# Fourth stage of a transformer kernel: products in three rounded parts instead of float32

## The reference

```python
topk_w, topk_idx = jax.lax.top_k(probs, TOP_K)
topk_w = topk_w / jnp.sum(topk_w, axis=-1, keepdims=True)
def expert_step(acc, ws):
    gw, uw, dw, ce = ws
    out = jax.nn.silu(x @ gw) * (x @ uw) @ dw
    return (acc + ce[:, None].astype(out.dtype) * out, None)
...
shared = jax.nn.silu(x @ s_gate_w + s_gate_b) * (x @ s_up_w + s_up_b) @ s_down_w + s_down_b
```

## Time and profile before

| | |
|---|---|
| median of three runs | 1208.76 us |
| profiled execution | 1218.6 us, span 1216.7 us |
| TensorE busy | 1056.7 us (87% of the span) |
| VectorE busy | 479.6 us (39%) |
| ScalarE busy | 341.5 us (28%) |
| GpSimd busy | 386.3 us (32%) |
| gate and up of the fourth stage, line 561 | 624 records, 193.2 us |
| down of the fourth stage, line 577 | 234 records, 107.1 us |

### The profile page before, as it was taken

The page is one execution under the profiler, slowest core; times in us unless marked ns, Lnnn a source line. Parts: engine busy times, 40 slices in busy tenths (PEclk is TensorE's granted clock), DMA queues, the critical chain, the costliest instruction groups (busy, mean ns, idle before and its releaser), DMA issues.

```text
span 1216.7 us, 13055 instructions
## 1 busy us (share of the span) xinstructions
PE 1056.7 (87%) x4351; PEld 705.6 (58%) x4351; DVE 479.6 (39%) x1148; ACT 341.5 (28%) x537; POOL 386.3 (32%) x340
## 2 busy tenths in 40 slices
PE   5886698979979989995599899999089999999996
PEld 4333243469869778884385657675055655565553
DVE  5678757333424544332854644515011111111110
ACT  3464141023323433332243332311012222221221
POOL 0004767525435445453002020202013332333232
PEclk9788699989989999997699999999589999999999
DMA  9111011179989998965406120209913323332330
GB/s 330 70 52 43 11 62 36 51 275 277 260 274 263 263 242 234 246 159 84 159 18 57 47 44 9 52 18 307 320 48 64 62 54 62 68 63 54 64 70 8
DMA packets 52800, 148.52 MB, mean 122 GB/s; under 512 B 12243, under 2 KB 12627, under 8 KB 47296
## 3 DMA queue, kind: packets, MB, share of 16 engines
q1 hardware_dynamic: 24752, 81.09, 21.0%
q0 software_dynamic: 24160, 44.03, 18.8%
q10 hardware_dynamic: 3824, 22.57, 5.8%
HBM read 109.76 MB, written 41.08 MB: 124 GB/s over the span
## 4 chain that ended last, share of the span: by engine, by line
PE 63%; DMA 16%; DVE 10%; issue 4%; ACT 3%; POOL 3%; ACTq 0%; SPq 0%; POOLq 0%; DVEq 0%
PE pb L561 15%; PE pb L577 8%; DMA acc_rows<-big 7%; PE pb L449 7%; PE pb L534 5%; DMA big<-hn_rows,big 5%; PE pb L308 4%; PE pb L310 4%; PE pb L309 4%; DVE big L874 4%; PE pb L315 3%; PE pb L403 3%; PE pb L371 3%; POOL acc_rows L1284 2%; DMA list_rows<-big 2%
## 5 line engine op out<-in xcount | busy, mean ns | idle before, releaser
L561 PE MATMUL pb<-big 128*128 x624 | 193.2, 463 | 4.1 <-issue 4.1
L449 PE MATMUL pb<-big 128*128 128x192 f32 x1024 | 174.1, 329 | 2.1 <-ACT bigr L721 1.3
L449 PEld LDWEIGHTS pb<-big 128*128 128x128 f32 x1024 | 169.8, 192 | 6.4 <-issue 3.4
L561 PEld LDWEIGHTS pb<-big 128*128 128x128 f32 x624 | 116.6, 192 | 63.4 <-issue 6.2
L1253 POOL DMA_INDIRECT list_rows<-big x96 | 95.8, 998 | 137.2 <-DVE big L886 108.5
L1284 POOL DMA_INDIRECT acc_rows<-big x64 | 95.4, 1491 | 138.2 <-DMA acc_rows<-big 53.5
L308 PE MATMUL pb<-bigr 128*128 128x512 f32 (+2 forms) x320 | 132.9, 415 | 7.0 <-DVE big L882 4.6
L1311 POOL DMA_INDIRECT out<-big x39 | 61.8, 1584 | 207.4 <-ACT big L854 207.4
L310 PE MATMUL pb<-bigr 128*128 128x512 f32 (+2 forms) x320 | 127.6, 399 | 0.0
L309 PE MATMUL pb<-bigr 128*128 128x512 f32 (+2 forms) x320 | 127.1, 397 | 0.0
L874 DVE TENSOR_TENSOR big<-big,pb 128x352 f32<-128x352 f32 (+4 forms) x87 | 33.4, 383 | 206.5 <-ACT big L848 192.4
(11 more groups left out here) (119 smaller groups left out, 1167.8 us busy)
## 6 DMA issues: line engine op xcount, KB each, us to landing
big<-in_we SPq DMA_DIRECT2D x32, 1024.0 KB, 8.0
rawr<-in_we SPq DMA_DIRECT2D x32, 512.0 KB, 4.4
big<-in_we ACTq DMA_DIRECT2D x1, 8704.0 KB, 41.5
hn_rows<-big SPq DMA_DIRECT2D x32, 256.0 KB, 2.0
big<-in_we ACTq DMA_DIRECT2D x1, 6528.0 KB, 54.4
big<-in_x SPq DMA_DIRECT2D x4, 1024.0 KB, 15.3
acc_rows<-big SPq DMA_DIRECT2D x16, 256.0 KB, 4.2
big<-acc_rows SPq DMA_DIRECT2D x16, 256.0 KB, 4.8
```

What stands on the lines that cost most here:

```text
L449: r = e.matmul(ps[:, m * CAP:(m + 1) * CAP], WR[b % 4][:, at_:at_ + 128], XT[b % 2][:, k, :], start=(k == 0), stop=(k == 3))
L561: r = e.matmul(ps[:, 0:I1], XT1[b % 2][:, k, :], W1[:, bass.ds(r0 + (q * 4 + k) * I1, I1)], start=(k == 0), stop=(k == 3))
```

## The change

Only the fourth stage is edited. ScalarE rounds each tile's operands and VectorE takes the remainders: the transposed tokens (`XH1`, `XL1`), the gate, up and down weights of the tile's expert (`wgh` and `wgl`, `wuh` and `wul`, `wdh` and `wdl`) and the transposed inner product (`NTH`, `NTL1`). There is one buffer for each of the weights' parts. The register is now loaded by ScalarE and by VectorE instead of TensorE. `upt` is cut in `gatet` and `upt`, and gate, up and down go through `three`. The gathers get a third buffer and semaphores of their own, and are issued three tiles ahead; many small tiles move to other places in SBUF. `IN1` is widened to 384 columns and its end zeroed (`zero4`), so that all three blocks have 128 rows.

```diff
-POOL_3 = "scatter1.0 scatter1.1 scatter1.2 scatter1.3 lists1 fetcht.0 fetcht.1"
+POOL_3 = "scatter1.0 scatter1.1 scatter1.2 scatter1.3 lists1 fetcht.0 fetcht.1 fetcht.2"
...
+        WGH, WGL = SLOT(RING + 9216, 4 * I1), SLOT(RING + 9216 + 4 * I1, 4 * I1)
+        WUH, WUL = SLOT(RING + 2048, 4 * I1), SLOT(RING + 2048 + 4 * I1, 4 * I1)
+        WDH1, WDL1 = SLOT(RING + 5120, 3 * D), SLOT(RING + 5120 + 3 * D, 3 * D)
...
-        pe4 = "turnt.0 " + words(lambda n: f"upt.{n} " + (f"turnt.{n + 1} " if n + 1 < NT else "") + (f"downt.{n - 1} " if n else "") + f"flipt.{n}", NT) + f" downt.{NT - 1}"
-        act4 = "turnt.0 " + words(lambda n: f"silut.{n} " + (f"turnt.{n + 1} " if n + 1 < NT else "") + (f"yt.{n - 1}" if n else ""), NT) + f" yt.{NT - 1}"
-        dve4 = words(lambda n: f"mult.{n} flipt.{n}", NT)
-        pool4 = words(lambda n: (f"fetcht.{n + 2} " if n + 2 < NT else "") + (f"addt.{n - 1}" if n else ""), NT) + f" addt.{NT - 1}"
+        pe4 = "turnt.0 " + words(lambda n: f"gatet.{n} upt.{n} " + (f"turnt.{n + 1} " if n + 1 < NT else "") + (f"downt.{n - 1} " if n else "") + f"flipt.{n}", NT) + f" downt.{NT - 1}"
+        act4 = "turnt.0 wgh.0 wuh.0 " + words(lambda n: f"silut.{n} " + (f"wgh.{n + 1} turnt.{n + 1} wuh.{n + 1} " if n + 1 < NT else "")
+                                              + (f"yt.{n - 1} " if n else "") + f"wdh.{n} flipt.{n}", NT) + f" yt.{NT - 1}"
+        dve4 = "zero4 turnt.0 wgl.0 wul.0 " + words(lambda n: f"mult.{n} " + (f"wgl.{n + 1} turnt.{n + 1} wul.{n + 1} " if n + 1 < NT else "")
+                                                    + f"wdl.{n} flipt.{n}", NT)
+        pool4 = words(lambda n: (f"fetcht.{n + 3} " if n + 3 < NT else "") + (f"addt.{n - 1}" if n else ""), NT) + f" addt.{NT - 1}"
...
-                    r0 = regs[b] = e.value_load(ETK[0:1, b:b + 1], min_val=0, max_val=7 * WE1)
-                    for q, ps in ((0, pg), (1, pu)):
-                        for k in range(4):
-                            r = e.matmul(ps[:, 0:I1], XT1[b % 2][:, k, :], W1[:, bass.ds(r0 + (q * 4 + k) * I1, I1)], start=(k == 0), stop=(k == 3))
-                    r.then_inc(s_pe, c.up())
+                elif kind in ("gatet", "upt"):
+                    q = 0 if kind == "gatet" else 1
+                    wh, wl = ((WGH, WGL), (WUH, WUL))[q]
+                    e.wait_ge(s_dve, dv("turnt", b))
+                    e.wait_ge(s_dve, dv("wgl" if q == 0 else "wul", b))
+                    if b >= 2:
+                        e.wait_ge(s_dve, dv("mult", b - 2))
+                    three(e, PB[2 + 2 * (b % 2) + q][:, 0:I1], [(XH1[b % 2][:, k, :], XL1[b % 2][:, k, :], wh[:, k * I1:(k + 1) * I1], wl[:, k * I1:(k + 1) * I1])
+                                                               for k in range(4)]).then_inc(s_pe, c.up())
...
+                elif kind in ("wgh", "wuh", "wdh"):
+                    at_, n, dst, user = dict(wgh=(0, 4 * I1, WGH, "gatet"), wuh=(4 * I1, 4 * I1, WUH, "upt"), wdh=(8 * I1, 3 * D, WDH1, "downt"))[kind]
+                    if b == 0:
+                        e.wait_ge(l_w1, 64)
...
+                    else:
+                        e.wait_ge(s_pe, pe(user, b - 1))
+                    if kind == "wgh":
+                        regs[b] = e.value_load(ETK[0:1, b:b + 1], min_val=0, max_val=7 * WE1)
+                    prev()
+                    e.activation(dst, w1[:, bass.ds(regs[b] + at_, n)], ACT.Copy).then_inc(s_act, c.up())
...
+                elif kind == "turnt":
+                    e.wait_ge(s_act, av("turnt", b))
+                    if b >= 2:
+                        e.wait_ge(s_pe, pe("upt", b - 2))
+                    tensor(XL1[b % 2].rearrange("p a b -> p (a b)"), PB[0][:, :], XH1[b % 2].rearrange("p a b -> p (a b)").bitcast(F32), ALU.subtract)
+                elif kind in ("wgl", "wul", "wdl"):
+                    at_, n, hi, lo, user = dict(wgl=(0, 4 * I1, WGH, WGL, "gatet"), wul=(4 * I1, 4 * I1, WUH, WUL, "upt"), wdl=(8 * I1, 3 * D, WDH1, WDL1, "downt"))[kind]
+                    e.wait_ge(s_act, av(kind[0:2] + "h", b))
+                    if b:
+                        e.wait_ge(s_pe, pe(user, b - 1))
+                    if kind == "wgl":
+                        regs[b] = e.value_load(ETK[0:1, b:b + 1], min_val=0, max_val=7 * WE1)
+                    tensor(lo, w1[:, bass.ds(regs[b] + at_, n)], hi.bitcast(F32), ALU.subtract)
...
-                    copy(NT1[b % 2][:, 0:2, :].rearrange("p a b -> p (a b)"), PB[1][:, 0:256])
-                    copy(NT1[b % 2][0:96, 2, :], PB[1][0:96, 256:384])
+                    e.wait_ge(s_act, av("flipt", b))
+                    tensor(NTL1[b % 2], PB[1][:, 0:384], NTH[b % 2].bitcast(F32), ALU.subtract)
```

More of the change, by code:

```diff
@@ L118, in program @@
         rawr = second_name("rawr", 17152, 34816, F32)
+        later = second_name("later", 38144, 53120, F32R)
+        slots = second_name("slots", 40192, 50176, F32R)
+        with nc.sbuf_tensor("w1", [128, 34816], F32) as w1:
+            pass
         big = ctx.enter_context(nc.sbuf_tensor("big", [128, 53120], F32))
@@ L133, in R, with LR, SLOT @@
             return S(off - 13056, *shape, mem=bigr)
+        def LR(off, *shape):
+            return S(off - 38144, *shape, mem=later)
+        def SLOT(off, *shape):
+            return S(off - 40192, *shape, mem=slots)
         def RAW(off, *shape):
@@ L227, in program @@
         SWD = late(6, D)
+        inter = late(6, D)
+        AC1 = [late(D) for _ in range(2)]
         SS1 = [late(D) for _ in range(2)]
-        AC1 = [late(D) for _ in range(2)]
         SB1, CC1 = late(12), late(4, 5 * E1)
@@ L239, in program @@
             c1.append(c)
-        ca = {"ST": late(4, 6), "MV": late(4, 2), "RS": late(4), "R2": late(4)}
-        recs = [(late(4, K1, 2), late(4, K1).bitcast(I32)) for _ in range(4)]
+        old = taker(CON_AT + C_TR, CON_AT + C_TR + T * K0)
+        recs = [(old(4, K1, 2), old(4, K1).bitcast(I32)) for _ in range(4)]
+        old = taker(CON_AT + C_INV, CON_AT + C_INV + 128)
+        ca = {"ST": old(4, 6), "MV": old(4, 2), "RS": old(4), "R2": old(4)}
         NB, NC, NTL = late(8), late(8), late(8)
         NI = late(8).bitcast(I32)
[L244 to L252, removed]
+        CMP, ETF, BLF = late(NT, 8), late(NT), late(NT)
+        ETK, BLI = old(NT).bitcast(I32), old(1).bitcast(I32)
+        assert late.at[0] <= RING + 9216 + 8 * I1
+        WGH, WGL = SLOT(RING + 9216, 4 * I1), SLOT(RING + 9216 + 4 * I1, 4 * I1)
+        WUH, WUL = SLOT(RING + 2048, 4 * I1), SLOT(RING + 2048 + 4 * I1, 4 * I1)
+        WDH1, WDL1 = SLOT(RING + 5120, 3 * D), SLOT(RING + 5120 + 3 * D, 3 * D)
+        NTH, NTL1 = ([LR(RING + 768 * i + 384 * q, 384) for i in range(2)] for q in range(2))
+        four = taker(RING + 9216 + 8 * I1, 53120)
+        XH1, XL1 = ([LR(four.at[0] + 1024 * i + 512 * q, 4, 128) for i in range(2)] for q in range(2))
+        four.at[0] += 2048
+        IN1 = [four(384), four(384)]
+        SL1 = [S(CON_AT + C_CM, I1), S(RING + 1536, I1)]
+        G1 = [S(CON_AT + NCONST + 512 * i, 512) for i in range(3)]
+        YS1 = [S(CON_AT + NCONST + 1536, 512), *AC1]
         mask_m = CON[:, C_CM:C_CM + 64].unsqueeze(1).broadcast_to([128, 8, 64])
@@ L268, in program @@
         l_g = [sem(f"l_gather{i}") for i in range(4)]
+        l_g4 = [sem(f"l_gathert{i}") for i in range(3)]
         l_rd = [sem(f"l_down{i}") for i in range(3)]
@@ L567, in _ @@
                     for k in range(3):
-                        w = 128 if k < 2 else 96
-                        r = e.transpose(PB[1][0:w, k * 128:(k + 1) * 128], IN1[b % 2][:, k * 128:k * 128 + w], ident)
+                        r = e.transpose(PB[1][:, k * 128:(k + 1) * 128], IN1[b % 2][:, k * 128:(k + 1) * 128], ident)
                     r.then_inc(s_pe, c.up())
@@ L574, in _ @@
                         e.wait_ge(s_act, av("yt", b - 2))
[L575 to L578, removed]
+                    e.wait_ge(s_dve, dv("wdl", b))
+                    three(e, PB[6 + b % 2][:, :], [(NTH[b % 2][:, k * 128:(k + 1) * 128], NTL1[b % 2][:, k * 128:(k + 1) * 128], WDH1[:, k * D:(k + 1) * D], WDL1[:, k * D:(k + 1) * D])
+                                                   for k in range(3)]).then_inc(s_pe, c.up())
                 assert c.n == pe(kind, *at), (kind, at)
@@ L583, in _ @@
             c = Counter()
+            regs = {}
             table = [None]
@@ L1227, in _ @@
                     both(AC1[j % 2], PB[j][:, :], TG[:, 3:4], xr[b][:, j, :], ALU.mult, ALU.add)
+                elif kind == "zero4":
+                    e.wait_ge(s_pe, pe_end3)
+                    for i in range(2):
+                        prev()
+                        e.memset(IN1[i][:, I1:384], 0.0).then_inc(s_dve, c.up())
+                elif kind == "turnt":
[11 more added lines that the diff above has]
+                    tensor(lo, w1[:, bass.ds(regs[b] + at_, n)], hi.bitcast(F32), ALU.subtract)
                 elif kind == "mult":
```

48 lines of the change are left out of this document (27 added, 21 removed).

## The result

The changed kernel takes **1331.24 us** (median, 1325.77 to 1341.26), beside 1210.49 (1204.76 to 1224.28) of the kernel before in the same comparison: a ratio of **1.102, interval 1.092 to 1.113**. The forecast was 1300 in a range of 1246 to 1345. The profiled execution is one of 1341.26 us, span 1339.5, against 1218.6 and 1216.7 before.

A forecast was written before the change was run, and what follows sets the result against it. TensorE bounds the kernel before at 8.08 us a tile; the change makes a loop of 10.3. 38 x 10.3, less 306.0, plus 3 and 2.7 is +91 us, added to the 1208.8 median: 1300 us, range 1246 to 1345.

The forecast's parts named there:

- The loop: Fourth stage, once a tile from `upt` over silu, `wgh`, `wgl`, `turnt` to gate and up: 9.40 us, 10.3 with the clock.
- VectorE's register load: Between `wgh` and `wgl`: the load follows the wait for `wgh`, so nothing covers it and it adds 0.76 us.
- The rival of hidden loads: Register loads hidden on both engines: loop 8.34 us, pause 1.8, +17 us, 1225 us; chance 0.08.
- ScalarE's register load: Before `wgh`: the load can run during the silu, so 0.30 of its 0.76 us stays on the loop.
- Rounded products at 352 columns: Gate and up on TensorE: 0.156 us a product, scaled from 0.227 at 512 columns; 24 take 3.74 us.
- The rival of a weight load that sets the pace: Gate and up: weight loads of 0.19 us pace the products, loop 10.2, 1297 us with the clock held; chance 0.05.
- The clock: TensorE after each pause: lower level taken at 0.6, costing 1.5 us of gate and up, so 0.9 a tile.
- The rival of the held clock: TensorE's clock holds through the pauses, so no 0.9 a tile: +57 us, 1266 us; chance 0.25.
- The pause: TensorE waits 2.85 us in every tile before gate: 5.66 outside gate and up, less 2.81 of other work.
- The ends: Start and end of the fourth stage: the first gate later, about +3 us; the tail after the last `upt` +2.7.
- What is late next: Work beside the loop: VectorE's sum 7.9 us a tile, ScalarE's 7.6, both under 9.4, so neither is the bound.
- The sum: Whole kernel: 38 x 10.3 = 391.4, less 306.0, plus 3 and 2.7, gives +91 us.

The follow-up runs named there:

- Experiment 3: Changed kernel with the next tile's `wgh` put before the silu and `wgl` before the multiplication: 1230.5 us, ratio 1.019 to the kernel before.
- experiment 1: Changed kernel with VectorE loading its register before it waits for `wgh`: 1286.81 us, ratio 1.071 to the kernel before.
- experiment 2: Changed kernel with 11 unused float32 products of 128 columns filling TensorE's pause in each tile: 1287.12 us, ratio 1.072 to the kernel before.
- experiment 4: Changed kernel with the order of Experiment 3 and both engines' register loads ahead of their waits: 1219.96 us, ratio 1.013 to the kernel before.
- experiment 6: Changed kernel with only down in three rounded products, gate and up back in float32: 1212.52 us, ratio 1.006 to the kernel before.
- experiment 8: Changed kernel with the gather of a later tile held for the `wgl` of two tiles before it: 1322.51 us, ratio 1.102 to the kernel before.

## Why the prediction was right, and where its sizes were off

- **The loop** (`upt`, silu, `wgh`, `wgl`, `turnt`, gate): right. Outside gate and up 5.66 was forecast and 5.71 measured, by the pieces `wgh` 1.38 (1.38), `wgl` 1.63 (1.63), `turnt` 0.69 (0.69). Experiment 3, which takes only the order away, gives back 2.31 us of a tile's added 2.81.
- **VectorE's register load, 0.76 and uncovered:** right. The wait for `wgh` cost 0.77 against 0.13 in experiment 1, and that gave back 0.73 outside gate and up. The rival of hidden loads is refuted.
- **ScalarE's register load, 0.30 left after the silu:** right in the mean and wrong in shape. `wgh` starts 0.18 after the silu in most tiles, 0.08 more than a plain gap, and 0.72 after it in 13, where the load takes 0.8. That the load can run while the silu executes is what was drawn from the Trainium skill (TensorE: Matmul & The Clock Gate, the table at its head); the trace agrees, as 0.18 after a silu is less than the 0.28 of the load itself.
- **Rounded products at 352 columns, 0.156:** measured 0.16 at full clock, 24 of them 3.83. Gate and up are 3.93 in the changed kernel at full clock, 0.19 more than the 3.74 of the sum: about half of it because the first product after a pause stands 0.26 ahead of the next (1017.77 to 1018.03), the rest in the other 23. The rival of a weight load that sets the pace is refuted. The estimate drawn from the Trainium skill (TensorE: Matmul & The Clock Gate, Part 3, what overlaps and what doesn't), 0.26 a pair, doesn't hold here either: the measured 0.16 decides.
- **The clock, 0.9 a tile: the term that was mis-sized.** A lower level was given to 0.6 of the pauses and 1.5 us to each. Measured: 25 of 38 tiles (0.66), and (5.15 - 3.93) x 38 / 25 = 1.85 us each, 1.22 over all tiles; by experiment 2, 1.16. The 3.0 us of lower level at the earlier trace rows were short for what comes here: the tile of 6.70 spent 6.0 us of gate and up at it (1005.57 to 1011.61). That the 0.66 lies near the 0.6 is partly luck, for the 0.6 was reasoned from the length of the pause, and pauses of 1.9 us in experiment 1 brought the lower level in more tiles (30) than those of 2.5 to 2.9. What decides it is not shown. The rival of the held clock is refuted, with a granted clock of 0.87 in the stage.
- **The pause, 2.85:** measured 100.5 us in 38 waits, 2.64, with VectorE's subtraction as the releaser, as forecast.
- **The ends:** the tail grew by 4.6 instead of 2.7. The start grew by 11.3 instead of 3, of which 8.1 is the later end of the weights in this one execution.
- **What is late next:** the sums of VectorE and ScalarE were rightly put under the loop. But VectorE's sum lies near the 8.05 of the kernel before: in experiment 4 it needed 8.04 for 6.86 of work, and no order that was tried made the whole change pay (8.31 a tile). The loop over the down weights (experiment 6) was not seen.
- **The sum** was +91 and the profiled spans differ by +122.8: the loop 21.5 more (of which the clock 0.32 x 38 = 12, gate and up 0.19 x 38 = 7, outside 2), the start 8.3, the tail 1.9. In the medians the kernel lost 120.8 us, 30 more than forecast; its 1331 lies inside the range. How the start stands in the executions that were not profiled is not known.

## What to carry to other kernels

Before a split or a copy is moved to an idle engine, follow the written order of that engine: work for the next tile that stands behind an instruction waiting for this tile makes a loop through all the engines, and its length, not the busy sums, is the time. Put such work ahead of the wait, and register loads ahead of it too where they stand on the loop: 0.71 us a tile for VectorE's alone here, but 0.24 for both together once the order was turned. Then add up each helper engine: here half of the change (gate and up only) was worth 2.4%, the whole of it cost 10%, and with the order mended still 1%.

## What the runs showed of the hardware that was not expected

- Pauses of 2.5 to 2.9 us once a tile (3.7 in one tile) brought the lower clock level in 25 of 38 tiles, and shorter ones of 1.85 to 2.0 in nearly all tiles of experiment 1 in 30 of 38. In experiment 3 two pauses a tile, none over 1.2 us, left the granted clock at 1.00. Eleven products that nobody needs took 0.86 us off each tile.
- ScalarE's load of one register from SBUF takes 0.28 us or longer, up to 0.97. In the changed kernel the slow ones (about 0.8) come right after the 13 tiles whose gate and up ran at full clock: there VectorE's subtraction from PSUM (`flipt`) still runs when the silu starts. When the clock was held (experiment 2) nearly all loads were slow, and 0.3 us of the 1.16 that the faster clock saved was lost that way. There it isn't the gather (experiment 8). Nor does a slow load need two engines reading PSUM at once: in experiment 3, 14 loads took 0.5 to 0.97 us while no ScalarE instruction ran and VectorE was at `wdl`, from SBUF to SBUF. A gather was being issued beside 13 of these 14, and beside one of the other 25. The cause stays open.
- A VectorE subtraction with an address in a register starts 0.24 us after the instruction before it, against 0.04 to 0.13 for the others.
